# A router's block on one core: where POOL issues seven loads of gate and up weights

## The reference, cut to what matters

```python
def _L0_attn_ref(hidden_states, Wq, Wk, Wv, Wo, gate):
    q, k, v = hidden_states @ Wq.T, hidden_states @ Wk.T, hidden_states @ Wv.T
    q = q * cos + rotate_half(q) * sin
    k = k * cos + rotate_half(k) * sin
    ...
    scores = jnp.einsum('bhqd,bhkd->bhqk', q, k) * scale
    attn = jnp.einsum('bhqk,bhkd->bhqd', jax.nn.softmax(scores, axis=-1), v)
    combined = g * mem_out + (1.0 - g) * attn
    return combined @ Wo.T

def _L0_ffn_ref(x, router_w, gate_w, up_w, down_w):
    top_v, top_i = jax.lax.top_k(logits, K)
    ...
    g = jnp.einsum('th,efh->etf', xf, gate_w)
    u = jnp.einsum('th,efh->etf', xf, up_w)
    y = jnp.einsum('etf,ehf->eth', jax.nn.silu(g) * u, down_w)
    out = jnp.einsum('te,eth->th', combine, y)

x = x + _L0_attn_ref(_layernorm(x), ...)
x = x + _L0_ffn_ref(_layernorm(x), ...)
```

## Time and profile before

| | us |
|---|---|
| median of 3 runs | 460.86 (460.09 to 462.53) |
| the profiled execution | 459.18 |
| its span | 456.9 |
| TensorE busy (matmuls) | 405.2 (89% of the span) |
| VectorE busy | 267.1 (58%) |
| ScalarE busy | 198.7 (43%) |
| POOL busy | 119.5 (26%) |
| POOL's DMA queue | 30.27 MB, 23.3% of 16 engines' span |
| SyncE's DMA queue | 15.96 MB, 13.6% |

### The profile page before, as it was taken

How to read it: one execution, slowest core, us unless ns; L and a number is a source line. 1 busy time by engine, 2 the same in 40 slices (tenths; PEclk the granted TensorE clock), 3 DMA queues, 4 the chain that set the end, 5 groups by cost and what they waited for, 6 DMA issues and landing times.

```text
span 456.9 us, 6506 instructions
## 1 busy us (share of the span) xinstructions
PE 405.2 (89%) x2144; PEld 204.0 (45%) x2145; DVE 267.1 (58%) x511; ACT 198.7 (43%) x349; POOL 119.5 (26%) x95
## 2 busy tenths in 40 slices
PE   0978889999729999999999999989999999999991
PEld 0526266222202222233242224467776567777761
DVE  7598997787706888768979911176423333233320
ACT  1237825676516667755756698421111111111110
POOL 6101746993001111000102610004621231212112
PEclk9998598999958999999999999999999999999997
DMA  6227655329973937100000248424331132221131
GB/s 199 100 91 153 147 94 106 104 85 293 344 217 116 313 108 255 35 0 1 1 1 1 95 135 299 155 69 171 83 48 36 26 45 48 35 35 26 21 105 23
DMA packets 24409, 48.15 MB, mean 105 GB/s; under 512 B 4448, under 2 KB 17888, under 8 KB 22528
## 3 DMA queue, kind: packets, MB, share of 16 engines
q0 software_dynamic: 7824, 30.27, 23.3%
q1 hardware_dynamic: 15984, 15.96, 13.6%
q10 hardware_dynamic: 576, 1.58, 1.0%
HBM read 30.05 MB, written 18.74 MB: 107 GB/s over the span
## 4 chain that ended last, share of the span: by engine, by line
PE 72%; DVE 13%; DMA 7%; issue 3%; ACT 2%; SPq 2%; POOL 1%; DVEq 0%; POOLq 0%; ACTq 0%
PE psum L1219 66%; DVE mem L945 7%; DMA mem<-mem 3%; PE psum L1483 3%; DMA parts_d<-mem 1%; DMA mem<-x 1%; ACT mem L775 1%; PE psum L1472 1%; PE psum L1343 1%; DVE mem L882 1%; PE psum L1256 1%; DVE mem L883 1%; SPq L419 1%; DMA mem<-parts_d 1%; SPq L432 1%
## 5 line engine op out<-in xcount | busy, mean ns | idle before, releaser
L1219 PE MATMUL psum<-mem 128*32 128x512 f32 (+11 forms) x1904 | 381.4, 460 | 29.0 <-DMA mem<-mem 11.6
L1219 PEld LDWEIGHTS psum<-mem 128*32 128x32 f32 (+5 forms) x1904 | 174.4, 135 | 213.6 <-issue 91.0
L945 DVE TENSOR_REDUCE mem<-psum 128x1 f32<-128x1024 f32 x128 | 151.8, 1218 | 43.1 <-PE psum L1219 42.6
L775 ACT ACTIVATE mem<-psum 128x512 f32<-128x512 f32 x256 | 137.8, 605 | 72.2 <-PE psum L1219 69.8
L644 POOL DMA_INDIRECT sum_d<-mem x18 | 28.1, 1563 | 84.8 <-ACT mem L793 59.3
L789 ACT ACTIVATE mem<-psum 128x688 f32<-128x688 f32 x18 | 13.4, 744 | 84.4 <-PE psum L1219 84.4
L1105 DVE COPY mem<-mem 128x3 f32<-128x3 f32 x18 | 3.2, 177 | 56.2 <-PE psum L1472 56.2
L1117 DVE COPY mem<-psum 128x512 f32<-128x512 f32 x18 | 12.4, 691 | 30.9 <-PE psum L1483 30.9
L793 ACT ACTIVATE mem<-psum,mem 128x256 f32<-128x256 f32 x18 | 8.5, 475 | 43.0 <-PE psum L1219 43.0
L598 POOL DMA_DIRECT2D xg_d<-mem x9 | 8.1, 899 | 54.2 <-PE psum L1219 54.2
L577 POOL TENSOR_TENSOR mem<-mem 128x64 f32<-128x64 f32 x2 | 21.1, 10556 | 4.1 <-ACT mem L752 4.1
(11 more groups left out here) (122 smaller groups left out, 205.3 us busy)
## 6 DMA issues: line engine op xcount, KB each, us to landing
mem<-gate_up POOLq DMA_DIRECT2D x8, 1376.0 KB, 9.9
xg_d<-mem POOLq DMA_DIRECT2D x8, 1036.0 KB, 8.8
mem<-down POOLq DMA_DIRECT2D x4, 1024.0 KB, 7.3
mem<-parts_d SPq DMA_DIRECT2D x24, 128.0 KB, 4.1
mem<-parts_d SPq DMA_DIRECT2D x48, 64.0 KB, 2.2
parts_d<-mem SPq DMA_DIRECT2D x18, 128.0 KB, 1.8
mem<-xg_d SPq DMA_DIRECT2D x16, 129.5 KB, 2.1
mem<-down POOLq DMA_DIRECT2D x2, 704.0 KB, 10.6
```

What stands on the lines that cost most here:

```text
L775: nc.scalar.activation(prob[:, t % 8], psum[:, score_bank(n, t)], ACT.Exp, scale=HD ** -0.5).then_inc(exp_ready, 1)
L945: V.tensor_reduce(mx[:, par, k:k + 1], banks(2 * (k % 2), 2), AX.X, ALU.max).then_inc(max_ready, 1)
L1219: return nc.tensor.matmul(*a, **k)
```

## The change

In the loop of L601 POOL no longer loads an expert's weights behind each second count. A new helper, `load_gate_up(e)`, first waits until the row of maxima of unit e + 1 has landed and then loads expert e. It is called in the loop at the odd experts (loads 0 to 3, once in each of the units 0 to 3), after `stage_v` of unit 5 (load 4, in unit 4), after `second_exp(0)` (load 5, in unit 5), and behind the first half's scatters (load 6, in unit 6 at the earliest, ahead of `load_down`). The fills, the waits of the loop and the load of the eighth expert stay.

```diff
+            def load_gate_up(e):
+
+                pool.wait_ge(mrow_in, 64 * (e + 2))
+                pool.dma_start(gu[:, e], gu_d[:, e]).then_inc(gu_in, 16)
+
             for e in range(E):
                 for m in range(2):
 
                     pool.wait_ge(av_ps, 4 * (e - e % 2) + 2 * (e % 2) + m + 1)
                     if m == 0:
                         fill(e * T, (e + 1) * T)
-                    elif e < E - 1:
-                        pool.dma_start(gu[:, e], gu_d[:, e]).then_inc(gu_in, 16)
-                    else:
-                        fill(E * T, NSLOT)
+                    elif e % 2:
+                        load_gate_up(e // 2)
+                        if e == E - 1:
+                            fill(E * T, NSLOT)
                 if e in (2, 4, 6):
                     u = e // 2 + 1
                     stage_v(u, u % 2, u % NQ)
             pool.wait_ge(av_ps, 8 * NQ)
             stage_v(NQ + 1, (NQ + 1) % 2, 1)
+            load_gate_up(NQ)
...
                 stage_v(u, u % 2, u % NQ)
                 if u == UNITS - 2:
                     second_exp(0)
+                    load_gate_up(NQ + 1)
             pool.wait_ge(xg_filled, 16 * (E + 1))
             scatter(0)
+            load_gate_up(NQ + 2)
```

## The result

The changed kernel took 444.9 us (median of 4 runs, 444.26 to 445.44), the kernel before 460.48 (4 runs, 459.79 to 462.53). The ratio is 0.9654 (95% interval 0.962 to 0.9688): 15.6 us less, where 13.9 were forecast. The profiled execution of the changed kernel took 445.17 us with a span of 443.3; for the profiled execution the forecast was 459.18 − 13.9 = 445.3. So the profiles agree with the sum within 0.1 us and the medians do not; both facts need an account. Part of the distance lies in the starting point: a fourth run, not yet there when the forecast was made, took the median of the kernel before from 460.86 to 460.48.

A forecast was written before the change was run, and what follows sets the result against it. The prediction took TensorE's wait for unit 2's row of maxima, behind POOL's queued fills and loads, as the bound. Median 460.86 − 13.9 (11.6 wait, the rest clock), moved parts at nothing, gave 447.0 us, range 445.6 to 450.3.

The forecast's parts named there:

- What bounds the kernel: Unit 2: TensorE waits 11.6 us for its row of maxima, late behind POOL's backlog of four fills and four loads.
- Load 0 stays in the crowd, the last fill at 121.5, the row just in time: Unit 2: four fills and load 0 stay ahead; row in at about 122.5 us, needed at 123.1, so no wait.
- late bound: Last fill ahead of unit 2's row lands at 122.9 us if each transfer costs 4.04 us whatever its size.
- the margin: Unit 2's row expected at about 122.5 us and needed at 123.1: 0.6 us, called thin.
- rival 1: Unit 2's row still a little late: 1.9 us of wait stay, 448.9 us; late, 450.3 or 452.6; chance 0.22.
- The inference from unit 3: Unit 3's row went out beside a fill and TensorE did not wait, so it needed less than 3.4 us behind it.
- The gain of unit 2: Unit 2 took 39.08 us against unit 3's 25.18, so 13.9 us to gain: 11.6 wait, the rest clock.
- All are costed at nothing: Moved loads 1 to 6, POOL's order and the delayed `dn` loads: all have cover, so cost 0 us.
- The step from the profile to the median: Median of the kernel before is 1.7 us above its profiled execution; carried over: 460.86 − 13.9 = 446.96.
- the low end: Range's lower limit, 445.6 us, from the scatter of the runs and a wait of later units not seen.
- The later loads in their new places: Loads 1 to 6 each land within about 10 us; `xg` has 4 us of cover; no delay.
- Rivals 2 to 4: 2: fills hold the row, 454.6 us (0.05); 3: load 6 delays `gate_up(0)`, 464 (0.02); 4: loads skip waits, 461 (0.03).

The follow-up runs named there:

- fills first: Kernel before with the same eight transfers ahead of unit 2's row, reordered to fills 0 to 3, then loads 0 to 3: 461.9 us, ratio 0.9953.
- two loads: Kernel before with loads 2 and 3 moved behind unit 2's row, leaving four fills and loads 0 and 1 ahead: 457.27 us, ratio 0.9837.
- none ahead: Changed kernel with each load one row later, so only four fills precede unit 2's row: 450.53 us, ratio 0.9688 to the kernel before.
- `stage_v` first: Kernel before with `stage_v` issued ahead of the same count's load at experts 2, 4 and 6: 463.7 us profiled; kernel before 465.02 median there.

## Why the prediction was right or wrong

Two terms of the sum failed. The gain of 13.9 us was put too low: the traces show 14.8, because the unit taken as a free one was not free and because the places that the loads left were costed at nothing. And the 1.7 us from the profiled execution to the median were carried over: the changed kernel showed −0.3. The mechanism of the wait was right.

**What bounds the kernel: right.** The row of maxima of unit 2 behind POOL's backlog was the wait, and the backlog as a whole, fills and loads, was its cause; the kernels with less or otherwise ordered traffic show it.

**Load 0 stays in the crowd, the last fill at 121.5, the row just in time: right in two profiles of four.** The forecast put the last fill 15.2 us behind the first `turn_o`, its late bound 16.6. It was in at 122.0, which is 14.5 us behind, and in the later profiles 15.3, 16.9 and 16.5. In the last two the row was late and TensorE idle for 0.9 and 0.6 us. So the margin was as thin as stated; rival 1 happened in small, at under 1 us, and not with its dip of the clock. The inference from unit 3 (a row needs less than 3.4 us behind its fill) pointed the right way, though the table shows that a row lands with the end of everything queued, loads too.

**The gain of unit 2: mis-sized.** I took 25.18 us, the length of unit 3, for a free unit. It was itself 0.43 us longer than the 24.75 of unit 2 in the changed kernel: 0.24 of that went with the change (25.18 to 24.94, next point), and 0.19 is between units 3 and 2 in the changed kernel too.

**"All are costed at nothing": wrong.** The moved loads had a cost on the chain in the kernel before: the issue of each load ahead of `stage_v` put POOL's copy onto VectorE's multiply, 0.25 us in each of units 1, 2 and 3. I looked for what the loads could do in their new places, and not for what POOL's next instruction gained when they left the old ones. The sum should have read 11.6 for the wait + 2.4 for the clock + 3 × 0.25 = 14.8, which is what the distances of `turn_o` show. That alone would have given 446.1 and put the low end at about 444.7, just under the 444.9 measured.

**The step from the profile to the median: wrong, and in the first measurement the larger error.** I carried the 1.7 us by which the median of the kernel before stood above its profiled execution over to the changed one. There it is not: 444.9 against 445.17. Later the kernel before stood above its own profiled execution by 1.4, and by 2.2 on the last chip (465.79 against 463.55). The changed kernel stood at −0.65, and on the last chip at −0.1 and at +0.65 (450.93 against 451.04 and 450.28). In the profiles with −0.65 and −0.1 unit 6 has the dip of the clock, about 1.5 us that another execution may not have. The kernels between them had 1.2 (fills first), 0.4 (two loads) and 1.5 (none ahead). So a wait of 9 to 12 us went with 1.2 to 2.2, and a wait of under 1 us or none with anything from −0.65 to 1.5; the offset is no constant, and one profile tells it to no better than that.

The mean granted clock of the timed executions points the same way in part: for the kernel before about 0.956 (0.954 to 0.963) where its profiles show 0.960 to 0.962, for the changed one 0.966 to 0.978 where its profiles show 0.965 to 0.971. A share missing from 1 is time at half speed, counted half: 2 × (1 − 0.956) × 462.5 = 40.7 us against 2 × (1 − 0.962) × 460.9 = 35.0, so 5.7 us more at the lower level. With the fills first it is the other way round: the two slowest runs (463.52 and 463.88 us) have 0.962, the rest 0.959. That the timed executions of the kernel before wait longer for the row than the profiled ones is therefore argued and not shown. The timed executions leave only span and clock, and where they differ stays open.

**Medians:** 15.6 us in the first measurement, 14.3, 14.5 (none ahead) and 14.9 in the others. The 14.8 us of the trace lie inside the interval of the first (0.962 to 0.9688 of 460.48 is 14.4 to 17.5 us). What the first measurement has above them, 0.8 us, is within what it can tell.

**The later loads in their new places: right.** Loads 1 to 6 landed in 5.9 to 7.4 us; the first `xg` was in at 263.6 (7.9 us after its issue), needed at about 266.2; from unit 4 to the end the two spans of the first pair are alike to 0.1 us. In the later profiles that part took 265.4 and 265.5 us in the kernel before and 266.9, 265.3 and 266.5 in the changed one; the two long ones are those with the dip in unit 6, which the kernel with `stage_v` first, with all loads in their old places, has too. Rivals 2 to 4 did not happen.

## What to carry to other kernels

When a transfer is moved, ask twice: what it does in its new place, and what the instruction that stood behind it does now that it starts sooner; the second was worth 0.75 us here and was left out. The length of a "free" stage should be taken from the shortest one or argued from its parts, since the neighbour used as a measure may carry costs of its own. An offset between one profiled execution and a median should not be carried over as a constant: over all kernels here it lay between −0.65 and 2.2 us, and the range must be open on that side too.

## What was not expected of the hardware

With eight transfers on POOL's queue a 2 KB transfer on SyncE's was in only 13 to 16 us after its issue, in either order of fills and loads; taking away 1376 KB that were queued behind everything else shortened its way by 5 us (15.6 to 10.6). And the clock: waits of 2.9 to 11.6 us all cost about the same 1.7 to 2.5 us behind them, a wait of 0.9 us only 0.2 (25.88 − 24.75 − 0.9). In unit 6 a wait of 1.8 us was followed by a stretch at 1.2 GHz in some profiles and not in others, for about 1.5 us. Last, POOL's copy beside VectorE: a multiply of 128x16 took 0.40 to 0.68 us instead of 0.18 when it fell into a copy of 128x512 on POOL.
